# Attention and mixture-of-experts block on one core: another order of TensorE's work in a half quarter

## The reference

```python
# cross attention: q = layernorm(x), k = v = ctx, SCALE = 1 / (8 * log(20))
s = SCALE * log(k_length)
attn = softmax(s * einsum('bhdq,bhdk->bhqk', qh, kh))
x = x + einsum('bhqk,bhdk->bhdq', attn, vh)
# experts: 2 of 8 for each of 2048 tokens
xt = layernorm(x)
probs = softmax(xt @ gate_w.T); weights, idx = top_k(probs, 2); weights /= weights.sum()
x = x + sum_a weights[a] * ((silu(xt @ w1[e].T) * (xt @ w3[e].T)) @ w2[e].T),  e = idx[a]
```

## Time and profile before

| what | value |
|---|---|
| profiled execution: span | 1285.3 us |
| profiled execution: its own time | not given beside the span; the runs' lowest is 1285.31 us |
| median of the runs | 1286.8 us |
| TensorE busy | 1125.7 us (88%), 5561 products |
| VectorE busy | 590.4 us (46%) |
| GpSimd busy | 606.7 us (47%) |
| ScalarE busy | 449.9 us (35%) |
| maxima (L682) | 256 at 1220 ns |
| exps (L559) | 512 at 598 ns |
| mean granted clock of TensorE | 0.957 |

### The profile page before, as it was taken

The page is one execution under the profiler, slowest core; times in us unless marked ns, Lnnn a source line. Parts: engine busy times, 40 slices in busy tenths (PEclk is TensorE's granted clock), DMA queues, the critical chain, the costliest instruction groups (busy, mean ns, idle before and its releaser), DMA issues.

```text
span 1285.3 us, 20411 instructions
## 1 busy us (share of the span) xinstructions
PE 1125.7 (88%) x5561; PEld 472.8 (37%) x5562; DVE 590.4 (46%) x884; ACT 449.9 (35%) x812; POOL 606.7 (47%) x547
## 2 busy tenths in 40 slices
PE   1899999999999999727999999999999999999810
PEld 0223333333333332213555554455455555544300
DVE  5877787877788875131222222222222222222245
ACT  3266666666666666611111111111111111111200
POOL 6434666666666541126504707428281473800045
PEclk9999999999999999958999999999999999999965
DMA  6454555555555441024203305124241333310157
GB/s 181 148 167 141 168 168 168 164 162 158 159 159 165 138 133 45 19 98 159 99 33 131 123 25 196 65 98 163 98 163 33 131 130 123 122 33 33 34 158 259
DMA packets 87243, 158.92 MB, mean 124 GB/s; under 512 B 13696, under 2 KB 52608, under 8 KB 81792
## 3 DMA queue, kind: packets, MB, share of 16 engines
q1 hardware_dynamic: 73728, 90.23, 22.9%
q0 software_dynamic: 12896, 67.12, 14.9%
q10 hardware_dynamic: 576, 1.05, 0.2%
HBM read 107.50 MB, written 50.86 MB: 123 GB/s over the span
## 4 chain that ended last, share of the span: by engine, by line
PE 75%; DVE 8%; DMA 6%; issue 5%; ACT 4%; POOL 2%; SPq 1%; DVEq 0%; POOLq 0%; ACTq 0%; PEldq 0%
PE rows L1048 30%; PE heads_out L1048 15%; PE heads_out L951 7%; PE scores L938 6%; PE rows L924 6%; ACT W L559 3%; DVE nm L682 3%; DMA W<-parts_dram 3%; PE scores L1081 2%; PE misc L1000 2%; DMA U<-expert_out_dram,fidx 1%; PE misc L1021 1%; PE misc L1040 1%; PE misc L977 1%; POOL U L523 1%
## 5 line engine op out<-in xcount | busy, mean ns | idle before, releaser
L1048 PE MATMUL rows<-W,U 128*128 x1776 | 392.1, 381 | 4.6 <-issue 3.0
L559 ACT ACTIVATE W<-scores 128x512 f32<-128x512 f32 x512 | 282.9, 598 | 160.2 <-PE scores L938 155.0
L682 DVE TENSOR_REDUCE nm<-rows 128x2 f32<-128x1024 f32 x256 | 305.5, 1220 | 58.3 <-PE rows L924 41.3
L1048 PEld LDWEIGHTS rows<-W,U 128*128 128x128 bf16 x1776 | 174.5, 98 | 208.9 <-issue 9.7
L1048 PE MATMUL heads_out<-W,U 128*128 x888 | 200.3, 383 | 5.2 <-issue 5.1
L924 PE MATMUL rows<-W,U 96*128 96x512 bf16 x512 | 163.7, 404 | 44.8 <-DMA W<-parts_dram 25.8
L865 DVE TENSOR_TENSOR U<-rows,U 128x512 f32<-128x512 f32 x78 | 53.8, 691 | 318.9 <-ACT U L627 318.9
L938 PE MATMUL scores<-U,W 128*128 128x512 bf16 x512 | 180.3, 387 | 13.9 <-ACT W L559 4.8
L400 POOL TENSOR_TENSOR W<-U,W 128x2048 bf16<-128x2048 f32 x42 | 171.0, 4072 | 7.7 <-POOL W L399 7.7
L627 ACT ACTIVATE U<-rows 128x512 f32<-128x512 f32 x78 | 46.4, 598 | 331.0 <-PE rows L1048 329.9
L951 PE MATMUL heads_out<-W,U 128*32 128x512 f32 x1024 | 138.0, 611 | 0.1
(11 more groups left out here) (144 smaller groups left out, 780.5 us busy)
## 6 DMA issues: line engine op xcount, KB each, us to landing
U<-wpack_dram POOLq DMA_DIRECT2D x42, 1024.0 KB, 5.2
parts_dram<-U SPq DMA_DIRECT2D x32, 384.0 KB, 4.1
U<-parts_dram SPq DMA_DIRECT2D x32, 384.0 KB, 3.9
W<-parts_dram SPq DMA_DIRECT2D x32, 384.0 KB, 5.1
U<-slots_dram SPq DMA_DIRECT2D x39, 256.0 KB, 2.6
expert_out_dram<-U SPq DMA_DIRECT2D x39, 256.0 KB, 2.1
parts_dram<-U SPq DMA_DIRECT2D x32, 256.0 KB, 3.9
stage<-wpack_dram POOLq DMA_DIRECT2D x12, 512.0 KB, 5.3
```

Source lines behind the costliest of these rows:

```text
L559: s.activation(probs[:, w % 2, j, kk, :], sc[u % 2][:, :], ACT.Exp) \
L682: v.tensor_reduce(nm[:, bb.parity, 2 * k:2 * k + 2], p1[k % 2][:, :].rearrange("p (c k) -> p c k", c=2), AX_X, ALU.max, negate=True).then_ ...
L1048: ins = m.matmul(bank, stat[:, s_part, k, :], W[:, bass.ds(at_w, 512)], start=(k == 0 and n == 0), stop=(k == n_chunks - 1 and n == 2))
```

## The change

In a half quarter TensorE's order becomes: two scores, two units, two scores, values. The small operations stand between these: z after the second pair of scores of (w = 0, part 0), gates after the units of (0, 1), v after the units of (1, 0), heads after the units of (1, 1), ranks after the second scores of (1, 1), maxima after the units of (3, 0), sums after the second scores of (3, 0). ScalarE's copies move by the same measure in its order: z transposed after four exps rather than three, the heads' sums after the first exp of the next quarter (rather than after the sixth of the same), v after two exps of quarter 1, picked heads after six. VectorE's order of maxima and small operations stays; two small operations come into `number`, which make the positions against which the experts' counts are compared, with -1 in place of 0 for the first, so that each expert has at least one tile.

```diff
--- before.py
+++ after.py
@@ -155,6 +155,7 @@
 
         tio_i = sb("tio_i", [P, T + 1], I32)
         tio = sb("tio", [P, 2, T + 1], F32)
+        tile_at = sb("tile_at", [P, B], F32)
         upto = sb("upto", [P, E, E], F32)
         tab = sb("tab", [P, 4, T + 1], I32)
         etab = sb("etab", [P, 2, E], I32)
@@ -567,33 +568,34 @@
                         act.wait_ge(S["sums_out"], bb.n * 32)
                     s.activation(og[:, gr, :], ob[:, :], ACT.Copy).then_inc(S["og_ready"], 1)
 
-                exps(0, range(0, 3))
+                exps(0, range(0, 4))
                 if pv2.within(0, B - 1):
                     act.wait_ge(S["zt_ps"], b.n - 1)
                     if b.within(3, B + 1):
                         act.wait_ge(S["gate_ready"], b.n - 2)
                     s.activation(zt[:, :, :].rearrange("p k t -> p (k t)"), misc[:, :], ACT.Copy) \
                         .then_inc(S["zt_ready"], 1)
-                exps(0, range(3, 6))
+                exps(0, range(4, 8))
+                exps(1, range(0, 1))
                 if pv.within(0, B - 1):
                     take_out(pv, 1)
-                exps(0, range(6, 8))
+                exps(1, range(1, 2))
                 if nb.within(0, B - 1):
                     act.wait_ge(S["vt_ps"], b.n + 2)
                     s.activation(vt[:, nb.parity, :, :, 0:DH], misc[:, :].rearrange("p (k h d) -> p k h d", k=4, h=H),
                                  ACT.Copy).then_inc(S["vt_ready"], 1)
-                exps(1, range(0, 4))
+                exps(1, range(2, 6))
                 if pv.within(0, B - 1):
                     act.wait_ge(S["u_ready"], b.n)
                     if pv.within(1, B - 1):
                         act.wait_ge(S["t_ready"], b.n - 1)
                     s.activation(us[:, :], misc[:, :], ACT.Copy).then_inc(S["us_ready"], 1)
-                exps(1, range(4, 8))
-                exps(2, range(6))
+                exps(1, range(6, 8))
+                exps(2, range(8))
+                exps(3, range(0, 1))
                 if full:
                     take_out(b, 0)
-                exps(2, range(6, 8))
-                exps(3, range(0, 5))
+                exps(3, range(1, 5))
                 if behind:
                     act.wait_ge(S["x1_ready"], b.n)
                     s.activation(xres[:, bass.ds(pv.n, 1), :].rearrange("p o q -> p (o q)"), x1[:, :], ACT.Copy) \
@@ -650,12 +652,14 @@
                 dve.wait_ge(S["consts"], N_CONST)
 
 
-                st = Steps(dve.wait_ge, S["table_chain"], 0, 5)
+                st = Steps(dve.wait_ge, S["table_chain"], 0, 7)
                 dve.wait_ge(S["numbered"], 1)
                 st.step(v.tensor_copy(tio[:, 0, :], tio_i[:, :]))
                 st.step(v.tensor_copy(numbers[:, :], tio_i[:, 0:E]))
                 st.step(v.tensor_scalar(first_rows[:, :], numbers[:, :], float(REG), None, ALU.mult))
                 st.step(v.tensor_scalar(tio[:, 1, :], tio[:, 0, :], float(P), None, ALU.mult))
+                st.step(v.tensor_copy(tile_at[:, :], tio[:, 1, 0:B]))
+                st.step(v.memset(tile_at[:, 0:1], -1.0))
                 st.step(v.tensor_tensor(upto[:, :, :], numbers[:, :].unsqueeze(2).to_broadcast([P, E, E]),
                                         numbers[:, :].unsqueeze(1).to_broadcast([P, E, E]), ALU.is_ge))
                 st.end()
@@ -795,7 +799,7 @@
             slots(dve, slot)
 
 
-            st = Steps(dve.wait_ge, S["table_chain"], 1, 5)
+            st = Steps(dve.wait_ge, S["table_chain"], 1, 7)
             link = st.step
             dve.wait_ge(S["pv_done"], 4 * B)
             link(v.tensor_tensor(gexp[:, :].unsqueeze(2), scores2[:, :, 1:2], scores2[:, :, 0:1], ALU.subtract))
@@ -811,7 +815,7 @@
             v.nop().then_inc(S["zero_ready"], 1)
 
             link(v.tensor_tensor(k3, cnt.unsqueeze(2).to_broadcast([P, E, B]),
-                                 tio[:, 1, 0:B].unsqueeze(1).to_broadcast([P, E, B]), ALU.is_gt))
+                                 tile_at[:, :].unsqueeze(1).to_broadcast([P, E, B]), ALU.is_gt))
             link(v.tensor_reduce(tiles, k3, AX_X, ALU.add))
             link(v.tensor_tensor(upto[:, :, :], upto[:, :, :], tiles.unsqueeze(1).to_broadcast([P, E, E]), ALU.mult))
             link(v.tensor_reduce(cum, upto[:, :, :], AX_X, ALU.add))
@@ -957,69 +961,91 @@
                 reader = (S["t_ready"], b.n - 1) if pv2.within(0, B - 1) else \
                     (S["m_ready"], b.n + 1) if full else None
 
+                def turn_z():
+                    pe.wait_ge(S["z_ready"], b.n - 1)
+                    pe.wait_ge(*reader)
+                    for k in range(KD):
+                        ins = m.transpose(misc[:, k * P:(k + 1) * P], z[:, b.parity, k * P:(k + 1) * P], ident[:, :])
+                    ins.then_inc(S["zt_ps"], 1)
+                    return S["zt_ready"], b.n - 1
+
+                def gates():
+                    pe.wait_ge(*reader)
+                    for k in range(KD):
+                        ins = m.matmul(misc[:, 0:E], zt[:, k, :], gw[:, k, :], start=(k == 0), stop=(k == KD - 1))
+                    ins.then_inc(S["gate_ready"], 1)
+                    return S["gate_used"], b.n - 1
+
+                def turn_v():
+                    pe.wait_ge(S["cv_in"], b.n * 16 + 32)
+                    if reader:
+                        pe.wait_ge(*reader)
+                    for kc in range(4):
+                        ins = m.transpose(misc[:, kc * P:(kc + 1) * P], cv[:, kc * P:(kc + 1) * P], ident[:, :])
+                    ins.then_inc(S["vt_ps"], 1)
+                    return S["vt_ready"], b.n + 2
+
+                def pick_heads():
+                    if reader:
+                        pe.wait_ge(*reader)
+                    pe.wait_ge(S["og_ready"], b.n * 2)
+                    for gr in range(2):
+                        ins = m.matmul(misc[:, :], selu[:, gr, :], og[:, gr, :], start=(gr == 0), stop=(gr == 1))
+                    ins.then_inc(S["u_ready"], 1)
+                    return S["us_ready"], b.n
+
+                def ranks():
+                    pe.wait_ge(*reader)
+                    pe.wait_ge(S["mask_ready"], b.n - 1)
+                    m.matmul(misc[:, 0:E], ltri[:, :], maskb[:, :], start=True, stop=False)
+                    m.matmul(misc[:, 0:E], onesb[:, :], mask_sum[:, :], start=False, stop=True) \
+                        .then_inc(S["rank_ready"], 1)
+                    return S["rank_used"], b.n - 1
+
+                def turn_maxima():
+                    pe.wait_ge(S["p1_used"], b.n * 16 + 32)
+                    if reader:
+                        pe.wait_ge(*reader)
+                    m.transpose(misc[:, 0:P], nm[:, nb.parity, :], ident[:, :]).then_inc(S["mt_ready"], 1)
+                    return S["m_ready"], b.n + 2
+
+                def spread_sums():
+                    pe.wait_ge(S["rec_in"], b.n * 16)
+                    if reader:
+                        pe.wait_ge(*reader)
+                    m.matmul(misc[:, :], selb[:, :], r8[:, :], start=True, stop=True).then_inc(S["r_ready"], 1)
+                    return S["t_ready"], b.n
+
+                routes = pv2.within(0, B - 1)
                 for w in range(4):
-                    for u in range(8):
-                        if u % 2 == 0:
-                            rows_unit(4 * w + u // 2)
+                    for part in range(2):
+                        u = 4 * part
                         if full:
                             score(w, u)
-                        if (w, u) == (0, 2) and pv2.within(0, B - 1):
...
+                            score(w, u + 1)
+                        rows_unit(4 * w + 2 * part)
+                        rows_unit(4 * w + 2 * part + 1)
+                        if (w, part) == (0, 1) and routes:
+                            reader = gates()
+                        if (w, part) == (1, 0) and ahead:
+                            reader = turn_v()
+                        if (w, part) == (1, 1) and behind:
+                            reader = pick_heads()
+                        if (w, part) == (3, 0) and ahead:
+                            reader = turn_maxima()
+                        if full:
+                            score(w, u + 2)
+                            score(w, u + 3)
+                        if (w, part) == (0, 0) and routes:
+                            reader = turn_z()
+                        if (w, part) == (1, 1) and routes:
+                            reader = ranks()
+                        if (w, part) == (3, 0) and behind:
+                            reader = spread_sums()
+                        if w == 0 and behind:
+                            values(pv, 3, part)
+                        if w > 0 and full:
+                            values(b, w - 1, part)
 
             slots(pe, slot)
             pe.wait_ge(S["og_ready"], 2 * B)
```

(29 more changed lines are left out.)

27 lines of the change are left out of this document (removed).

## The result

The changed kernel takes 1345.2 us (median of 4 runs, 1344.21 to 1349.41) against 1287.28 for the kernel before: ratio 1.0452, 95% interval 1.0428 to 1.0476. The direction was as forecast; 1322 was 23 us short, and 1345.2 lies 4 us above the upper end of the range. The profiled execution has a span of 1347.7 us; it is the longest of the four (1349.41 us), so sums over its trace come out some 4 us above the median. In every run the span is 1.5 to 1.7 us shorter than the time of the same execution.

The account below looks back on a forecast made before the run. Each slot was taken as bound by TensorE with score stalls, then by a VectorE chain from gates to row unit 5. 1285.3 + 25.5 (slots +28.6, start -3.5, small operations +0.4) + 12 (clock) = 1322.8, said 1322; range 1292 to 1341.

Parts of the forecast that it names:

- Step 1: Ordinary half quarter on TensorE: 2.9 us instead of 3.32, a gain of 0.4 us.
- Step 2: Gates to row unit 5: TensorE work beside VectorE's chain falls 4.55 to 2.40 us; wait grows 1.0 to 2.5-3.
- the masks' excess: VectorE's masks took 0.17 to 1.11 us; half the excess removed gave chain 5.1 us, full price 5.5.
- Step 3: TensorE from row unit 5 to the gates' end: 3.0 us of stalls, 28.2 us instead of 25.53.
- the walk: One slot of the new order laid over profiled durations: 33.3 us, 2.2 more than 31.09.
- the masks at full price: Slot estimate if VectorE's masks keep their full stretched length: chain 5.5 us, slot 33.6 us.
- Step 4: DMAs (heads' reload, reciprocals, maxima) stay hidden, reload with 1.3 us to spare; uncovered, at most 1 us a slot.
- Step 5: Slot 0 and the beginning of slot 1, without routing, gain 3.5 us; the last slots change by 0.
- Step 6: Two more small VectorE operations in the numbering, 0.2 us each: +0.4 us, bounds 0.2 to 1.
- Step 7: TensorE's clock halves behind unit 5's stop in two slots of three, 1.4 us each: +12 us, bounds 0 to 21.
- D: Rival: clock falls in every slot and slows the pieces between too, 1332 to 1341 us; chance 0.15.

Follow-up runs that it names:

- experiment 5: Kernel before, only the gate products moved later, from behind score (0, 4) to behind score (0, 6): 1318.53 us, ratio 1.0248.
- experiment 2: Changed kernel with the gate products ahead of row units 2 and 3 instead of behind them: 1330.29 us, ratio 1.0325.
- experiment 6: Changed kernel with row unit 5 moved behind the values of (1, 0) instead of beside unit 4: 1318.45 us, ratio 1.0248.
- experiment 7: Changed kernel with gates ahead of row units 2 and 3 and unit 5 behind the values of (1, 0): 1301.53 us, ratio 1.0115.
- experiment 3: Changed kernel with ScalarE's copy of x1 behind the last exp of quarter 3 instead of the fifth: 1345.21 us, ratio 1.0441.
- experiment 1: Changed kernel with twelve throwaway products issued between row units 4 and 5 of each slot that routes: 1327.36 us, ratio 1.0311.
- experiment 4: Changed kernel with row units 0 and 1 of each slot ahead of its first two scores: 1349.86 us, ratio 1.0486.
- (12): Changed kernel with TensorE's former order up to slot 0, the new one from slot 1, ScalarE's order new throughout: 1345.7 us, ratio 1.045.
- 11: Kernel before with row unit 5 moved behind the picking of the heads, from ahead of score (1, 2): 1274.04 us, ratio 0.9885.
- experiment 10: Changed kernel, gates and maxima's transposes sooner, unit 5 later, sums' spreading before (3, 0)'s last score, x1 copy last: 1294.17 us, ratio 1.0044.

## Why the prediction was right and wrong

- *Step 1* (ordinary half quarter 2.9 us) was right: in slot 0, where nothing else stands, values follow each other at 65.87, 68.79, 71.74 and 74.62, 2.88 to 2.95 us.
- *Step 2*, the step that decides the sign, was right: a wait of 2.69 us in the mean (1.38 to 3.55) against 2.5 to 3, seen in the trace, and shown by taking it away from either side. Moving the gates alone costs the old order 30 us (5), giving back work to the shadow returns 15 (2), 27 (6) and 44 us (7). Its size was off in one choice: I took half of the masks' excess away, chain 5.1. From the gates' end to unit 5 it is 5.5 in the mean, since other small operations of the row took the delay: 0.4 x 13, some 5 us.
- *Step 3* (stalls between unit 5 and the gates) came out near in sum, wrong in parts. Foreseen and there: ranks 0.26 (0.4 said), unit 11 0.36 (0.45), score behind the sums' copy 0.26 (0.4). z waited 0.2 instead of 0.8, unit 1 not at all; in their place stood a wait that the walk had missed, 0.91 us of the last score of (3, 1), whose exp is queued on ScalarE behind the copy of x1 and so behind GpSimd. Experiment 3 shows that these are not separate costs: without the one, z and unit 1 wait for as much. With the clock held up the slot is 33.80; the walk said 33.3, the masks at full price 33.6.
- *Step 4* held: from 94 to 555 us no TensorE operation of the changed kernel waits for a DMA.
- *Step 5* failed: "-3.5 us" up to slot 1, measured +5.4 in the profiled execution. In experiments 1, 2 and 3, with the same order up to there, it was +2.5, +2.9 and +1.8. The difference between these four is in large part when the clock rises (a pair of scores lasts 1.06 us ahead of the rise, 0.60 behind it): at 64.6 us in the profiled execution of the changed kernel, at 58.5, 59.2 and 56.2 in the three, at 58.4 before. So the order alone does not make the late rise; the same order had it early three times. What all four have is the other part: the half quarters of slot 0 did gain, but the walk began where scores already run, and the first scores of slots 0 and 1, which now stand ahead of the units, wait for the maxima's DMA (at slot 1 1.73 us here, 1.55 to 1.72 in the three):

```profile
54.87 1.01 PE L942 MATMUL scores<-U,W 128*128 128x512 bf16 x2 [0.35 <-DMA U<-maxima_dram]
...
83.91 0.60 PE L942 MATMUL scores<-U,W 128*128 128x512 bf16 x2 [1.73 <-DMA U<-maxima_dram]
```

 I had checked that DMA for a routed slot of 33 us; slot 0 lasts 29, and there the cover is gone. Neither reordering (4) nor TensorE's former order (12) brought the time back, so how much of it that wait is worth by itself stays open.
- *Step 6*: the numbering on VectorE took 2.89 us instead of 2.44 in the trace, the 0.4 said; the two new operations themselves last 0.18 and 0.06.
- *Step 7* was right in kind and failed in size: two slots of three at 1.4 us, 12 us in all. The clock fell in 13 of 13 slots, four times for twice as long, and experiment 1 prices it at 18 us in the medians, 21 in the profiled executions. Of the rivals D, the clock falling in every slot (1332 to 1341), came nearest.

So the mechanism that sets the sign was right, and three terms of the sum were too small: the clock of step 7, the chain's length of step 2, and the start of step 5, which had even the wrong sign. In the profiled executions the sum closes. The spans differ by 62.4 us where 37.5 were forecast (1322.8 less 1285.3). Of the 24.9 missing, the clock is 8.7 (20.7 against 12), the slots with the clock up 8.2 (13 x 2.83 = 36.8 against 28.6), the start 8.9 (+5.4 against -3.5), and the rest -0.8. Against the medians less is missing, since this execution was 4 us longer than the median of its kernel; experiments 1 to 3 put 2.5 to 3.6 us of that at the start. And some 1.6 us of the 23 are no term of the kernel: the sum began at a span, 1285.3, and is compared with a time, which is 1.5 to 1.7 us longer than the span. By the same difference the profiled execution of the kernel before took some 1286.9 us, about its median (an estimate; its own time is not on record), and was not 1.5 us below it.

The sentence on the skill's rule (the Trainium skill, TensorE: Matmul & The Clock Gate, "HAM oscillation — how this bites in real kernels"), that a recurring wait can throttle each turn anew, gave 21 for this term. The trace of the changed kernel agrees in each of the 13 slots; with the same stop the clock fell in 12 slots in experiment 3. The 18 to 21 us of experiment 1 are nearer to it than my 12. With 21 the forecast would have been 1331, still 14 us short.

## What to carry to other kernels

Where one engine runs a short chain that another waits for, count the work that is written between its trigger and its consumer. Here 4.55 us of it left 1.00 us of a chain of 5.55 uncovered, and some 2.6 us left 2.83 (in the slot shown), whatever the rest of the order gained. The cheapest repair found here was to move the consumer: one row unit moved in the old order gave 1.1%. A stop of TensorE that comes back in every turn can cost twice, once as itself and once as the clock behind it: here the clock was 18 of the 58 us. A price taken from the slowest execution's trace carries what only that execution had, as the start did here.

## What the runs showed of the hardware

- In the changed kernel stops of 1.4 to 3.55 us, one in each slot, went with a granted clock of 0.50 in 13 of 13 slots. The same stops did so in 12 in experiment 3, stops of 0.9 to 2.6 us in 10 (experiment 2), of 1.4 to 3.1 in 10 (experiment 4). The length of the stop alone did not decide it: the clock stayed up behind one of 3.06 us (experiment 4) and fell behind one of 1.38 (the changed kernel).
- In experiment 5 the clock fell in seven slots, in six of them at two waits of about 0.7 us within 1.3 us, in one behind a wait of 2.51. In experiment 6 it fell in four, three times behind a wait of 1.57. In experiments 7 and 11, with waits of 0.5 us and less around the gates, it stayed up in all 13 slots, in experiment 10 in all but one, and in the kernel before up to slot 13 with one wait of 0.6 to 1.2 us a slot. The stretches were 3.4 or 6.8 us long.
- Twelve products whose result is thrown away, issued into that stop, made the kernel 18 us faster.
- A small VectorE operation of 0.16 to 0.17 us was stretched to as much as 1.1 us when it began beside one of GpSimd's 128x512 operations, and then ended 0.01 to 0.04 us behind it, in 50 of 50 cases of this chain in the traces before and after. Which operation it hits goes by the moment: masks 1.01 before, the copy of 2 columns 1.05 after, a cast 1.11 in experiment 7. That GpSimd's operation is the cause was not tried by a run.
